# A graph layer on one core: group 0 normalised ahead of the flag, copies on VectorE from group 31, finer signals at the end

## The chip, the cores and the metric

The kernel runs on one core of a Trainium2 chip. The metric is the device time of one execution in microseconds. Three executions of the kernel before took 3143.07, 3151.29 and 3159.94 us; the median is 3151.29 us.

## What is computed

```python
h = relu(layernorm(x))                          # x: 12500 x 256, f32
agg = segment_sum(h[src], dst)                  # 200000 edges drawn, 12500 nodes
z = (1 + eps_gin) * h + agg
t = relu(batchnorm(z @ W1 + b1, g1, bt1))       # 12500 x 512
out = x + relu(batchnorm(t @ W2 + b2 + h, g2, bt2))
```

The edges are sorted by dst. Layernorm is by row; batchnorm takes its mean and variance over all 12500 rows, so that nothing of its output can be made before all of its input is there. All is f32.

## The kernel before, in words

**Tiling.** The edges are cut into 1563 tiles of 128 edges, and these into 196 groups of 8 (the last has 3). A group's rows of h are gathered into SBUF, VectorE makes a 0/1 selection matrix for it (`selection`, L712: edges x a window of 96 nodes), and TensorE sums rows into the window with 8 tiles in 16 matmuls (`aggregate`, L1228). The window is copied out of PSUM (`keep_window`, L1062), transposed (L1238) and added by VectorE into the transposed sums `aggT` (`add_window`, L789). Nodes are cut into 98 node tiles of 128, one for two groups: h of a node tile is loaded, transposed on TensorE (`transpose_h`, L1254), VectorE makes z from it (`z_tile`, L820), and the transposed h is copied over the sums, which are no longer needed (`keep_hT`, L1055). Four node tiles make a chunk of 512 nodes, 25 in all, the last of 212. `times_W1` (L1263) multiplies a chunk in 4 blocks of 128 features, one in each of four steps out of eight; `t_and_b1` (L1071) adds b1 on the way from PSUM to the buffer `tb`, VectorE takes its statistics (`t_stats`, L828), and SP stores t to DRAM (`store_t`, L451).

**Who gathers.** POOL gathers a tile of 128 rows with one indirect DMA (L606). It waits for `s_agg`, the count of summed groups, since there are 4 row buffers. In 31 groups SP fetches the eighth tile itself, row by row: it loads 16 addresses into registers (L477, a piece) and issues 16 transfers of one row of 1 KB (L482). In 24 groups from 39 on ScalarE does the same for the seventh tile (L1098, L1102). Up to group 29 the rows are those of x, and statistics, root, scale, shift and `normalise` (L1014, ScalarE) are applied to each group. Meanwhile ScalarE and VectorE also normalise x in 25 batches and store h to DRAM; from group 30 on all gathers read h (`wait_h`).

**Order.** Each engine runs its own list in the order of the code. The loop variable g of `step(g)` runs over the groups on TensorE, VectorE and ScalarE, each with its own offsets; the last four groups are written out by hand. SP's list is a loop over the 98 node tiles, here called passes: `load_node_tile(c)` (L446), which waits until node tile c - 2 has been transposed, in every fourth pass `store_t` (L451), and then the pieces of its tile, 11 quarters of a piece in a pass on average. In pass 1 it waits for the first `add_window`. ScalarE issues 5 quarters of a piece in each step, ahead of its copies of that step.

**Flag.** Early on, VectorE computes whether all edges lie within their windows (`flag`, L738). PE, ACT, POOL and DVE read it and would run a slow general path if it were 0. Group 0's statistics are taken before that and its scale, shift and normalisation after it.

**The end.** After the last sums, batchnorm 1 is finished (L933 to L942), ScalarE makes relu of a chunk (`relu1`, L1176), TensorE multiplies it by W2 in 2 blocks of 8 matmuls (`times_W2`, L1345), and VectorE adds b2 and h and takes statistics (`y_chunk`, L950 and L956). Then batchnorm 2, relu (L1187), transposes (L1359), the sum with x (`residual`, L972), and the store (L568). `keep_warm(n, bank)` (L1301) are n multiplications of the identity with itself whose result nobody reads.

```python
            def keep_window(w):                        # ScalarE
                act.wait_ge(s_agg, w + 1)
                if w >= 2:
                    act.wait_ge(s_wT, w - 1)
                S.copy(win_sb[w % 2], win_ps[w % 2]).then_inc(s_ev, 1)
...
                if c >= 2:                             # SP, load_node_tile
                    if c - 2 < H_NODES:
                        sp.wait_ge(s_hx, c - 1)
                    else:
                        sp.wait_ge(s_hT, c - 1)
```

## Time and profile before

| | before |
|---|---|
| median of three executions | 3151.29 us |
| profiled execution, its own time | 3149.71 us |
| its span, first to last instruction | 3147.9 us |
| mean granted TensorE clock | 0.72 |
| PE busy | 1454.9 us (46%) |
| POOL busy | 1431.3 us (45%) |
| VectorE (DVE) busy | 632.1 us (20%) |
| ScalarE (ACT) busy | 472.7 us (15%) |
| DMA moved | 325.72 MB, 103 GB/s |

In a profile PE is the matmuls, PEld the weight loads, and a name with q (SPq, ACTq) is an engine's queue in its role as issuer of DMAs, which isn't counted as busy. "Idle before ... <-" tells what ended an engine's idle time before an instruction: an instruction of another engine, a DMA, "issue" when the engine's queue was at something that isn't counted as busy (issuing DMAs, loading registers, fetching), and "remote" when no releaser was found. PEclk is the clock that TensorE was granted, as a share of full speed.

### The profile page before, as it was taken

To read this page: it belongs to the slowest core of one execution; us is meant where nothing else is said; L and a number is where in the kernel's file an instruction comes from. 1 tells how busy PE (TensorE), PEld (TensorE's weight loads), DVE (VectorE), ACT (ScalarE), POOL (GpSimd) and SP (SyncE) were. 2 spreads that over 40 slices of the span, in tenths; PEclk is the share of its full clock that TensorE was granted. 3 is DMA by queue.
4 is the path that set the end of the run, shared out by engine and by line. 5 is a ranking of instruction groups with operands and counts; after the bars stand their busy time and mean duration, and the time that the engine had idled before them with its cause. 6 is when DMAs were issued, how large, how long until landed. Compare 5 with 4: busy or idle time off the path is not lost.

```text
span 3147.9 us, 31339 instructions
## 1 busy us (share of the span) xinstructions
PE 1454.9 (46%) x4883; PEld 918.7 (29%) x4883; DVE 632.1 (20%) x1628; ACT 472.7 (15%) x979; POOL 1431.3 (45%) x1518
## 2 busy tenths in 40 slices
PE   2443444444434434443352453344444253444999
PEld 2222222333222222232231232222223132322546
DVE  6454531111101101111011011011011010111346
ACT  4553530000000000000000000000000000000445
POOL 5645455555444453454344544544544454553000
PEclk7766677776776776776676766767766666767999
DMA  5544432332222222222222322222322222233646
GB/s 162 169 142 145 135 111 87 93 100 79 86 87 71 87 87 78 85 87 80 75 73 84 96 71 80 83 82 87 93 74 80 76 90 80 79 92 120 235 161 255
DMA packets 129207, 325.72 MB, mean 103 GB/s; under 512 B 35641, under 2 KB 61594, under 8 KB 122862
## 3 DMA queue, kind: packets, MB, share of 16 engines
q0 software_dynamic: 72384, 197.75, 21.3%
q1 hardware_dynamic: 43946, 99.32, 8.8%
q10 hardware_dynamic: 12676, 26.68, 2.6%
q14 instruction: 162, 1.33, 0.1%
q8 instruction: 39, 0.64, 0.1%
HBM read 271.56 MB, written 52.05 MB: 103 GB/s over the span
## 4 chain that ended last, share of the span: by engine, by line
SPq 47%; issue 28%; PE 8%; ACTq 2%; another core or an unknown queue 0%; DVE 0%; ACT 0%; DVEq 0%; DMA 0%
SPq L482 38%; SPq L477 8%; PE ps L1345 5%; ACTq L1102 2%; PE ps L1359 1%; SPq L446 1%; PE ps L1301 0%; PE ps L1228 0%; PE ps L1263 0%; SPq L467 0%; SPq L451 0%; ACTq L1098 0%; DVE aggT L789 0%; DVE st L632 0%
## 5 line engine op out<-in xcount | busy, mean ns | idle before, releaser
L606 POOL DMA_INDIRECT arena<-h_rows,arena x1272 | 1205.4, 948 | 1262.9 <-PE ps L1228 755.7
L1228 PE MATMUL ps<-arena 128*96 128x256 f32 x3016 | 940.1, 478 | 754.1 <-issue 217.9
L1228 PEld LDWEIGHTS ps<-arena 128*96 128x96 f32 x3016 | 624.2, 212 | 1047.0 <-issue 619.9
L1254 PE MATMUL ps<-ident,arena 128*128 128x128 f32 x196 | 55.6, 381 | 668.7 <-ACT aggT L1055 357.5
L606 POOL DMA_INDIRECT arena<-in_x,arena x220 | 208.5, 948 | 197.2 <-PE ps L1228 112.6
L828 DVE BATCH_NORM_STATS2 arena<-arena 128x6 f32<-128x512 f32 x92 | 63.7, 693 | 1080.4 <-ACT arena L1071 788.9
L1254 PEld LDWEIGHTS ps<-ident,arena 128*128 128x128 f32 x196 | 26.8, 183 | 717.9 <-issue 685.3
L789 DVE TENSOR_TENSOR aggT<-aggT,ps 128x192 f32 x196 | 69.4, 354 | 739.6 <-PE ps L1238 357.4
L1263 PE MATMUL ps<-arena 128*128 128x512 f32 (+3 forms) x412 | 209.9, 639 | 1.3 <-DVE arena L820 1.1
L1062 ACT COPY arena<-ps 96x256 f32<-96x256 f32 x196 | 71.8, 367 | 899.1 <-issue 688.6
L1055 ACT COPY aggT<-ps 128x256 f32<-128x256 f32 x98 | 36.0, 369 | 1039.6 <-issue 1025.6
L712 DVE TENSOR_TENSOR arena<-arena,ps 128x768 f32<-128x768 f32 x196 | 185.5, 947 | 19.6 <-PE ps L1228 19.5
L1238 PE MATMUL ps<-ident,arena 96*128 96x96 f32 x392 | 68.2, 256 | 234.9 <-DVE aggT L789 180.5
L1345 PE MATMUL ps<-arena,W2s 128*128 128x512 f32 (+1 forms) x400 | 167.8, 582 | 0.0
L1014 ACT ACTIVATE arena<-arena,nb,mv 128x256 f32<-128x256 f32 x236 | 119.2, 587 | 203.5 <-DVE nb L700 127.8
L1238 PEld LDWEIGHTS ps<-ident,arena 96*128 96x128 f32 x392 | 54.8, 146 | 267.3 <-issue 228.9
L1071 ACT ACTIVATE arena<-ps,prmT 128x512 f32<-128x512 f32 (+1 forms) x100 | 67.5, 677 | 381.6 <-DMA t_T<-arena 327.9
L820 DVE SCALAR_TENSOR_TENSOR arena<-ps,eps,aggT 128x256 f32<-128x256 f32 x98 | 46.9, 480 | 364.8 <-remote 138.4
L1345 PEld LDWEIGHTS ps<-arena,W2s 128*128 128x128 f32 x400 | 75.8, 190 | 91.8 <-issue 85.9
L1263 PEld LDWEIGHTS ps<-arena 128*128 128x128 f32 x412 | 77.5, 210 | 55.7 <-issue 53.4
L632 DVE BATCH_NORM_STATS2 st<-arena 128x6 f32<-128x256 f32 x236 | 80.6, 409 | 52.1 <-DMA rl_odd<-in_x 37.8
L1176 ACT ACTIVATE arena<-arena,sh,sc 128x512 f32<-128x512 f32 (+1 forms) x100 | 72.1, 793 | 92.0 <-PE ps L1345 91.1
(94 smaller groups left out, 532.8 us busy)
## 6 DMA issues: line engine op xcount, KB each, us to landing
rl_odd<-h_rows SPq DMA_DIRECT2D x3456, 1.0 KB
W2s<-h_rows ACTq DMA_DIRECT2D x3072, 1.0 KB
t_T<-arena SPq DMA_DIRECT2D x24, 1024.0 KB, 3.8
arena<-t_T SPq DMA_DIRECT2D x24, 1024.0 KB, 4.8
arena<-h_rows,arena POOLq DMA_INDIRECT x1272
arena<-in_x SPq DMA_DIRECT2D x27, 512.0 KB, 5.6
h_rows<-arena ACTq DMA_DIRECT2D x24, 512.0 KB
out<-arena SPq DMA_DIRECT2D x23, 512.0 KB
```

The costliest lines, as they stand in the source:

```text
L477: sp.reg_load(regs, sp_at[j % 2][0:1, m * PIECE:(m + 1) * PIECE])
L482: sp.dma_start(sp_rows[j % ROW_BUFS][e:e + 1, :].bitcast(mybir.dt.uint8), a[bass.ds(at, ROW_BYTES)].rearrange("(p e) -> p e", p=1)).then_i ...
L606: nc.gpsimd.indirect_dma_start(out=rows[slot(g)][:, k, :], out_offset=None, in_=(x if g < H_FROM else h_dram)[:, :], in_offset=bass.Indire ...
L632: last = V.bn_stats(o, r)
L712: V.tensor_tensor(sel[:, g % 2, :, :], rel[:, g * GT:(g + 1) * GT].unsqueeze(2).to_broadcast([P, GT, W]), iota_ps.unsqueeze(1).to_broadcas ...
L1014: last = S.activation(rows_of(g, k), rows_of(g, k), ACT.Relu, bias=nb[:, g % 2, k:k + 1], scale=mv[:, g % 2, k, 1:2])
L1176: S.activation(u[:, k % 2, f, 0:n], tin[:, k % 2, f, 0:n], ACT.Relu, bias=sh1[:, f:f + 1], scale=sc1[:, f:f + 1]).then_inc(s_u, 1)
L1228: last = T.matmul(win_ps[g % 2], sel[:, g % 2, k, :], rows_of(g, k), start=k == 0, stop=k == n - 1)
L1238: last = T.transpose(winT_ps[:, f, :], win_sb[w % 2][:, f * P:(f + 1) * P], ident[0:W, 0:W])
L1254: last = T.transpose(hT[:, f, 0:n], h[0:n, f * P:(f + 1) * P], ident[0:n, 0:n])
L1263: last = T.matmul(t_ps[(FB * q + m) % TB][:, a:b], W1s[:, k, m * P:(m + 1) * P], zt[q % 2][:, k, a:b], start=k == 0, stop=k == DB - 1)
L1345: last = T.matmul(c_ps[k % 2][m][:, 0:n], W2s[:, f, m * P:(m + 1) * P], u[:, k % 2, f, 0:n], start=f == 0, stop=f == FB - 1)
```

## The change

- Group 0: `inverse(0)` and `shift(0)` follow `mean_and_var(0)` on VectorE, and ScalarE runs `normalise(0)` ahead of its wait for the flag; step 1 no longer holds them.
- From step 31 (`COPIES_FROM`) on `keep_window`, `keep_hT` and `t_and_b1` run on VectorE in place of ScalarE, each at its place in VectorE's step: the window copy first, the bias before the selection, the copy of hT right after the z tile. ScalarE's list has only its row issues there. The last groups, written out by hand, keep these copies on ScalarE, which waits for VectorE's last ones.
- The store of t's chunk 23 goes out after the last `add_window` in place of before it.
- `s_c` (products with W2) and `s_y` (their sums) count blocks in place of chunks.
- The last chunk's sum with x, and its store, are made in two halves.
- `keep_warm` between the last sums and the first product with W2: 4, 1, 6 and 12 in place of 8, 3, 10 and 26.
- The pieces of a pass are counted in eighths, 22 and 10, in place of quarters, 11 and 5.

```diff
@@ -37,11 +37,12 @@
 X_EARLY = 16
-SP_QUARTERS = 11
-ACT_QUARTERS = 5
+SP_EIGHTHS = 22
+ACT_EIGHTHS = 10
 H_FROM = 30
...
 HB = 4
+COPIES_FROM = H_FROM + 1
 LAST = 4
@@ -93,26 +94,26 @@
-        def quarters(q, n):
-            return q * n // 4
+        def eighths(q, n):
+            return q * n // 8
...
         while True:
-            done = ceil(4 * per_tile * (len(sp_groups) + 1), SP_QUARTERS)
+            done = ceil(8 * per_tile * (len(sp_groups) + 1), SP_EIGHTHS)
             if done > H_NODES or 2 * (done - 1) + 6 >= H_FROM:
...
         while True:
-            done = ceil(4 * per_tile * (len(sp_groups) - SP_X + 1), SP_QUARTERS) + H_NODES
+            done = ceil(8 * per_tile * (len(sp_groups) - SP_X + 1), SP_EIGHTHS) + H_NODES
             if 2 * (done - 1) + 6 >= NG - 4:
...
         while True:
-            done = ceil(4 * per_tile * (len(act_groups) + 1), ACT_QUARTERS) + H_ACT
+            done = ceil(8 * per_tile * (len(act_groups) + 1), ACT_EIGHTHS) + H_ACT
             if done - 1 + 4 >= NG - 4:
@@ -490,9 +492,9 @@
                 if c < H_NODES:
-                    return row_pieces(quarters(SP_QUARTERS, c), quarters(SP_QUARTERS, c + 1), SP_X)
+                    return row_pieces(eighths(SP_EIGHTHS, c), eighths(SP_EIGHTHS, c + 1), SP_X)
                 c -= H_NODES
-                return [(SP_X + j, m) for j, m in row_pieces(quarters(SP_QUARTERS, c), quarters(SP_QUARTERS, c + 1),
+                return [(SP_X + j, m) for j, m in row_pieces(eighths(SP_EIGHTHS, c), eighths(SP_EIGHTHS, c + 1),
                                                             len(sp_groups) - SP_X)]
@@ -527,8 +529,8 @@
             sp.dma_start(W2s[:, :, :], W2.rearrange("(k p) n -> p k n", p=P)).then_inc(s_w, 16)
+            sp.wait_ge(s_add, NG)
             store_t(NQF - 1)
-            sp.wait_ge(s_add, NG)
             for q in range(X_FIRST):
@@ -553,8 +555,8 @@
                                  (in_0, in_1, s_u, FB * (last[0] + 1)),
-                                 (at_u + 2, in_0, s_c, last[1] + 1),
-                                 (at_u, at_u + 2, s_c, last[0] + 1)):
+                                 (at_u + 2, in_0, s_c, DB * (last[1] + 1)),
+                                 (at_u, at_u + 2, s_c, DB * (last[0] + 1))):
                 for i in range(m, end):
@@ -567,9 +569,14 @@
                                  x_place(i)[a:b, :, :]).then_inc(s_o, 16)
-            for i in range(NQ):
+            for i in range(NQ - 1):
                 store_out(i)
-            sp.wait_ge(s_o, 16 * sum(len(row_parts(last_order(i)[1])) for i in range(NQ)))
+            q, n = last_order(NQ - 1)
+            for b in (0, 1):
+                sp.wait_ge(s_sum, NQ + b)
+                sp.dma_start(out[q * QN:q * QN + 4 * n, :].rearrange("(p b k) d -> p b (k d)", b=2, k=2)[:, b, :],
+                             x_place(NQ - 1)[:, b, :]).then_inc(s_o, 16)
+            sp.wait_ge(s_o, 16 * (2 + sum(len(row_parts(last_order(i)[1])) for i in range(NQ - 1))))
@@ -717,6 +724,8 @@
             mean_and_var(0)
+            inverse(0)
+            shift(0)
@@ -855,14 +864,39 @@
+            def keep_hT(c):
+                n = rows_of_node_tile(c)
+                dve.wait_ge(s_zt, c + 1)
+                dve.wait_ge(s_hTc, c)
+                hT = hT_ps if c < NT - 1 else hT_last
+                V.tensor_copy(aggT[:, :, c * P:c * P + n], hT[:, :, 0:n]).then_inc(s_hTc, 1)
+
+            def keep_window(w):
+
+                dve.wait_ge(s_agg, w + 1)
+                dve.wait_ge(s_ev, w)
+                dve.wait_ge(s_wT, w - 1)
+                V.tensor_copy(win_sb[w % 2], win_ps[w % 2]).then_inc(s_ev, 1)
+
+            def t_and_b1(q, m):
+                dve.wait_ge(s_t, FB * q + m + 1)
+                if m == 0:
+                    dve.wait_ge(s_td, 16 * q)
+                dve.wait_ge(s_tst, FB * (q - 1) + m + 1)
+                dve.wait_ge(s_tb, FB * q + m)
+                V.tensor_scalar(tb[:, m, :], t_ps[(FB * q + m) % TB][:, 0:QN], b1T[:, m:m + 1], None, ALU.add
+                                ).then_inc(s_tb, 1)
+
             def step(g):
+                if g >= COPIES_FROM:
+                    keep_window(g - 2)
                 if 2 <= g < H_FROM:
...
                     statistics_node_tile((g - 4) // 2)
-                if g <= H_FROM:
+                if 2 <= g <= H_FROM:
                     inverse(g - 1)
@@ -872,7 +906,7 @@
                     mean_and_var_node_tile((g - 4) // 2)
-                if g <= H_FROM:
+                if 2 <= g <= H_FROM:
                     shift(g - 1)
@@ -883,9 +917,14 @@
                     add_window(g - 4)
+                q, m = divmod(g - 2 * PG * Q + 1, PG * Q)
+                if g >= COPIES_FROM and m < FB:
+                    t_and_b1(q, m)
                 selection(g)
...
                     z_tile((g - 7) // 2)
+                    if g >= COPIES_FROM:
+                        keep_hT((g - 7) // 2)
                 if g - 1 < NQ:
@@ -944,13 +983,12 @@
                 n = QN if q < NQF else TAILN
-                dve.wait_ge(s_c, q + 1)
                 for f in range(DB):
+                    dve.wait_ge(s_c, DB * q + f + 1)
                     y = aggT[:, f, q * QN:q * QN + n]
-                    last = V.scalar_tensor_tensor(y, c_ps[q % 2][f][:, 0:n], b2T[:, f:f + 1], y, ALU.add, ALU.add)
-                last.then_inc(s_y, 1)
-                dve.wait_ge(s_y, q + 1)
-                for f in range(DB):
+                    V.scalar_tensor_tensor(y, c_ps[q % 2][f][:, 0:n], b2T[:, f:f + 1], y, ALU.add, ALU.add
+                                           ).then_inc(s_y, 1)
+                    dve.wait_ge(s_y, DB * q + f + 1)
                     at = 3 + 6 * (q - AHEAD2)
@@ -969,7 +1007,12 @@
                 dve.wait_ge(s_oT, i + 1)
-                V.tensor_tensor(x_place(i, n), o_ps[i % 2][0:n, :, :], x_place(i, n), ALU.add).then_inc(s_sum, 1)
+                if i < NQ - 1:
+                    V.tensor_tensor(x_place(i, n), o_ps[i % 2][0:n, :, :], x_place(i, n), ALU.add).then_inc(s_sum, 1)
+                else:
+                    for b in (0, 1):
+                        z = x_place(i, n)[:, b, :]
+                        V.tensor_tensor(z, o_ps[i % 2][0:n, b, :], z, ALU.add).then_inc(s_sum, 1)
             for i in range(NQ):
@@ -1073,6 +1116,7 @@
             zero_step(2)
+            normalise(0)
             act.wait_ge(s_flag, 1)
@@ -1112,27 +1156,27 @@
                     load_batch(g)
-                if g <= H_FROM:
+                if 2 <= g <= H_FROM:
                     normalise(g - 1)
...
                 if g >= H_ACT:
-                    for j, m in row_pieces(quarters(ACT_QUARTERS, g - H_ACT), quarters(ACT_QUARTERS, g - H_ACT + 1),
+                    for j, m in row_pieces(eighths(ACT_EIGHTHS, g - H_ACT), eighths(ACT_EIGHTHS, g - H_ACT + 1),
                                            len(act_groups)):
...
                         root_node_tile((g - 4) // 2)
-                    if g >= 8:
+                    if 8 <= g < COPIES_FROM:
                         keep_hT((g - 8) // 2)
-                if g >= 2:
+                if 2 <= g < COPIES_FROM:
                     keep_window(g - 2)
...
                 q, m = divmod(g - 2 * PG * Q + 1, PG * Q)
-                if q >= 0 and m < FB:
+                if q >= 0 and m < FB and g < COPIES_FROM:
                     t_and_b1(q, m)
@@ -1142,8 +1186,10 @@
+            act.wait_ge(s_ev, a - 2)
+            act.wait_ge(s_hTc, c - 1)
+            act.wait_ge(s_tb, FB * q + 1)
             keep_window(a - 2)
-            keep_hT(c - 2)
             t_and_b1(q, 1)
@@ -1171,7 +1217,7 @@
                 if at_least(q, 2):
-                    act.wait_ge(s_c, q - 1)
+                    act.wait_ge(s_c, DB * (q - 1))
                 for f in range(FB):
@@ -1324,27 +1370,27 @@
             pe.wait_ge(s_tb, FB * NQF - TB + 1)
-            keep_warm(8, idle)
+            keep_warm(4, idle)
             aggregate(a + 3)
-            keep_warm(3, idle)
+            keep_warm(1, idle)
             transpose_window(a + 3)
-            keep_warm(10, idle)
+            keep_warm(6, idle)
             for m in range(FB):
                 times_W1(NQF, m)
-            keep_warm(26, 1)
+            keep_warm(12, 1)
...
             def times_W2(q, k, r, n=QN):
-                if at_least(q, 2):
-                    pe.wait_ge(s_y, q - 1)
                 for m in range(DB):
+                    if at_least(q, 2):
+                        pe.wait_ge(s_y, DB * (q - 2) + m + 1)
                     for f in range(FB):
...
                                         start=f == 0, stop=f == FB - 1)
-                last.then_inc(s_c, 1)
+                    last.then_inc(s_c, 1)
             chunks(pe, 4, NQF, times_W2, lambda q, k, r: times_W2(q, k, r, TAILN))
```

## Rows read from the trace of the kernel before

**Rows 1.** Busy time by engine in one stretch (number of instructions behind x)
```profile
core 0: us, PE busy (x) PEld busy (x) DVE busy (x) ACT busy (x) POOL busy (x), PEclk, DMA share, GB/s
...
522.40:2877.60 2355.20, 984.96 (x3254) 631.54 (x3254) 278.20 (x467) 130.44 (x311) 1140.68 (x1204) 0.69 0.28 83
```
**Rows 2.** The page's chain by line, and SP's own waits in the whole span
```profile
SPq L482 38%; SPq L477 8%; PE ps L1345 5%; ACTq L1102 2%; PE ps L1359 1%; SPq L446 1%; PE ps L1301 0%; PE ps L1228 0%; PE ps L1263 0%; SPq L467 0%; SPq L451 0%; ACTq L1098 0%; DVE aggT L789 0%; DVE st L632 0%
...
SPq L446 <- DVE aggT L789: 26.6, 1, 26.6
...
SPq L446 <- PE ps L1254: 9.7, 1, 9.7
```
**Rows 3.** Stretches from one node-tile load to the next: POOL's gathers (L606)
```profile
1141.09:1184.28 43.19, 28.89 (x31) 0.73 0.33 97
2308.72:2336.04 27.32, 17.14 (x19) 0.80 0.30 89
2336.04:2365.23 29.19, 15.66 (x17) 0.68 0.28 83
2402.52:2424.16 21.64, 0.00 (x0) 0.50 0.17 64
2611.37:2646.53 35.16, 17.21 (x19) 0.79 0.24 70
2823.21:2864.79 41.58, 28.26 (x30) 0.66 0.34 99
```
**Rows 4.** Waits from 530 to 2877 us, and L1062's group there
```profile
PE ps L1254 <- ACT aggT L1055: 343.1, 36, 21.5
...
PE ps L1228 <- ACT arena L1062: 157.5, 27, 15.4
...
L1062 ACT COPY arena<-ps 96x256 f32<-96x256 f32 x157 | 57.8, 369 | 855.2 <-issue 667.0 <-PE ps L1238 95.5 <-remote 80.8
```
**Rows 5.** Timeline: start, us, row issues and a gather; L1102's first and last start
```profile
1154.89 11.52 ACTq L1102 DMA_DIRECT2D W2s<-h_rows  x17
...
L1102 ACTq DMA_DIRECT2D W2s<-h_rows x3072: 2/235/1412, 444.9 to 2748.2; - x192
...
2310.40 10.23 SPq L482 DMA_DIRECT2D rl_odd<-h_rows  x14
...
2319.93 5.63 SPq L482 DMA_DIRECT2D rl_odd<-h_rows  x3
...
2332.18 0.95 POOL L606 DMA_INDIRECT arena<-h_rows,arena  x1 [3.71 <-remote]
...
2337.69 8.87 SPq L482 DMA_DIRECT2D rl_odd<-h_rows  x16
```
**Rows 6.** Timeline: a wait for a t store, and the last such store
```profile
2407.08 0.69 ACT L1071 ACTIVATE arena<-ps,prmT 128x512 f32<-128x512 f32 x1 [23.31 <-DMA t_T<-arena]
...
2878.99 0.43 SPq L451 DMA_DIRECT2D t_T<-arena  x1
...
2889.51 0.69 ACT L1071 ACTIVATE arena<-ps,prmT 128x512 f32<-128x512 f32 x1 [34.76 <-DMA t_T<-arena]
```
**Rows 7.** Timeline: the flag, the first sums, the fifth gather, the first window added
```profile
46.66 0.14 DVE L738 TENSOR_SCALAR flag<-flag_f 1x1 int32<-1x1 f32 x1 [9.55 <-remote]
...
55.08 5.46 PE L1228 MATMUL ps<-arena 128*96 128x256 f32 x16 [20.63 <-ACT arena L1014]
...
61.35 0.94 POOL L606 DMA_INDIRECT arena<-in_x,arena  x1 [16.92 <-PE ps L1228]
...
84.12 0.35 DVE L789 TENSOR_TENSOR aggT<-aggT,ps 128x192 f32 x1 [7.39 <-remote]
```
**Rows 8.** Timeline: warming, first relus, first products with W2
```profile
2929.68 5.97 PE L1301 MATMUL ps<-ident 128*128 128x128 f32 x52
...
2932.38 5.75 ACT L1176 ACTIVATE arena<-arena,sh,sc 128x512 f32<-128x512 f32 x8 [0.84 <-DVE sh L942]
...
2935.49 25.06 PE L1345 MATMUL ps<-arena,W2s 128*128 128x512 f32 x58
```
**Rows 9.** Timeline: sums of the tail chunk, and the last residual
```profile
3103.36 0.78 DVE L950 SCALAR_TENSOR_TENSOR aggT<-ps,prmT,aggT 128x212 f32<-128x212 f32 x2
...
3142.08 1.23 DVE L972 TENSOR_TENSOR aggT<-ps,aggT 128x1024 f32<-128x1024 f32 x1 [0.18 <-PE ps L1359]
```

More of the change, by code:

```diff
@@ L200, in build @@
         W1s = piece[1].rearrange("p (k n) -> p k n", n=F)
+        assert COPIES_FROM % 2 == 1 and COPIES_FROM > max(H_ACT, 2 * H_NODES + 2, NQ + 2)
         W2s = sb("W2s", [P, FB, D])
```

## The prediction

> **What bounds the kernel now.** I read the stages first, then which queue never waits, then what slows that queue. The gather stage runs from 452.6 to 2877.6 us; in its 2355 us from 522.4 on PE is busy 42%, VectorE and ScalarE 12% and 6%, and POOL, the highest, 48% of the time [rows 1]. No engine is full. The chain of waits puts 38% of the span on SP's queue at L482, the issue of one-row transfers [rows 2]. SP's own waits confirm it: two matter, 26.6 us for the first window sum and 9.7 us for a transpose of TensorE, and in the stretch 522.4 to 2877.6 us there is none [rows 2]. So SP is never late because of anyone: whoever else waits there waits in SP's shadow.
>
> What sets SP's pace is seen by cutting the stage into passes (node-tile load to node-tile load, two groups each, 32 or 48 one-row transfers, 2.75 pieces of 16 on average). A pass of 48 rows takes 21.64 us when POOL gathers nothing in it, 35.16 us with 19 gathers, 41.58 and 43.19 us with 30 and 31; one of 32 rows takes 27.32 us with 19 [rows 3]. That is (41.58 - 21.64) / 30 = 0.66 us for a gather and 21.64 / 48 = 0.45 us for a row. The diff leaves both counts as they are: 22 eighths of a piece are 11 quarters, 10 eighths are 5 quarters. So the stage keeps its length unless SP begins to wait or the gathers fall otherwise in time.
>
> **ScalarE's copies.** From group 31 VectorE takes over 157 window copies of 369 ns and the copies and biases at L1055 and L1071. TensorE now waits 343.1 us for L1055 and 157.5 us for L1062 there [rows 4], because these copies stand behind bursts of row issues in ScalarE's queue. Those 500 us go, but TensorE then waits for the next node tile or SP's rows, which come no sooner: worth nothing on the path. VectorE has room for the copies, some 140 us of busy time in a stretch in which it is busy 278 of 2355 us [rows 1, 4]. What does come off is SP's own wait: its pass due at 512.4 us starts at 522.4 because TensorE's transpose waits for L1055 and L1062 behind ScalarE's issues. **Minus 9.7 us** [rows 2]; bounds 0 (something else holds the transpose) and 9.7.
>
> ScalarE, freed, issues its rows with fewer pauses. The trace shows whether that robs SP: the pass of 43.19 us had 31 gathers and 17 rows of ScalarE in one row of the timeline alone, the pass of 41.58 us had 30 gathers and came after ScalarE's last row at 2748.2 us [rows 3, 5]. Less the one gather of 0.66 us, 0.95 us is left for at least 17 rows, at most 0.06 us each; ScalarE's total stays the same, so I take nothing. The Trainium skill ("DMA: Bandwidth & Descriptors", section "Issuing engines are not separate DMA queues") says that transfers of all issuers end on the same 16 engines and interleave; if ScalarE's rows cost SP as much as SP's own, the two passes should lie 17 x 0.45 = 7.7 us apart, and they lie 1.61 us apart.
>
> **The wait that moves to VectorE.** The bias of block 0 waits until the previous t store has landed, and SP issues that store only at the start of a later pass. ScalarE stood 23.31 us in such a wait [rows 6], and VectorE's statistics stand behind it even now. Now VectorE itself stands there, and selection of group 8q+15, the z tile and the copy of hT are queued behind it; TensorE misses one group more before the block ends, and POOL one release. SP asks for a transpose two node tiles back, so it has about two passes (60 us) of slack against a delay of about one group (some 10 us of gathers): nothing, 19 times. The last block has no pass after it: the store goes out at 2878.99 behind two 1 MB loads and ScalarE resumes at 2889.51 [rows 6]; selection of group 191 now waits for that, where its sums ran at 2886. Between 0 and 5 us, of which later stalls of up to 6 us may hide part: **plus 2 us**.
>
> **Group 0.** Its normalisation comes after the flag (46.66 us), and TensorE's first sums start at 55.08 after 20.63 us of waiting; POOL's fifth group then starts at 61.35 after 16.92 us [rows 7]. Normalised before the flag (ScalarE is free from 30 us), the sums can start about 49 us, so POOL starts 6 us sooner. The groups after it gain less, since VectorE's scale and shift for group 1 come only 0.4 us sooner. SP's second pass hangs on the first window sum at 84.12 [rows 7] and nothing but transfers follows it, so what arrives there is kept: between 0 and 6, **minus 4 us**.
>
> **Warming.** 26 calls are 52 matmuls of L1301 and take 5.97 us, 0.23 us each [rows 8]. The first four calls removed lie between sums (-0.9 us); of the next, two are hidden behind the last window copy; four before W1 give 0.6 us until the z tiles are there; 14 of the last 26 calls would give 3.2 us, but the first product can't precede the first of 8 relus, which start at 2932.38 and take 0.72 us each, where TensorE started at 2935.49 [rows 8]: -2.3 us. **Minus 3.8 us**, if the clock stays at the 1.00 of that stretch; if it fell to half for the first chunk, 6.7 us of products would cost 6.7 more.
>
> **Small ends.** Signals per block let VectorE take block 0 of the tail chunk while TensorE makes block 1: the first of the two sums (0.78 us for both) and its statistics, a little shorter, go beside it: **-0.6 us** [rows 9]. For the other chunks TensorE never waits, so nothing. The last residual takes 1.23 us before its store [rows 9]; in halves the first store goes out 0.6 us sooner, the second carries half as much but VectorE pays a second start of some 0.1 us: -1.1 to +0.3, **-0.5 us**. The t store behind the last sums is needed at chunk 6 at the earliest: 0.
>
> **Sum.** The profiled execution took 3149.7 us (span 3147.9), the median is 3151.3. -9.7 + 2 - 4 - 3.8 - 0.6 - 0.5 = -16.6: **3133 us**, 0.58% under the median. A measurement of this kernel can tell about 0.5% from no change, so the borders are 3135.5 and 3167.0 us, and the forecast lies just past the first.
>
> **Rivals.**
> 1. *Gathers broken up more.* SP's cost for a gather isn't constant: two passes of 48 rows took 29.19 us with 17 gathers and 35.16 us with 19 [rows 3]. Before and within the first POOL stopped between groups, once for 3.71 us, and SP issued 16 rows in 8.87 us; in a long stretch of gathers it issued 14 rows in the first 10.23 us and then 3 in 5.63 us [rows 5]. Long unbroken stretches cost SP more. If TensorE at SP's heels leaves POOL in catching-up mode, in which it breaks after every 8 gathers, I let one of 8 of the 79 passes turn from unbroken to split: 10 x 5 = -50 us (5 us is the 5.97 between the two passes less 2 gathers at the 0.44 of a split pass, (29.19 - 21.64) / 17): 3083 us.
> 2. *Slower: gathers bunched.* The same rows in the other direction. ScalarE's bursts of rows now space TensorE's groups, and POOL, which waits for each, gathers in pieces. With prompt copies two groups follow each other closely, and POOL can gather 16 tiles without a break in each pass. It decides if more than about one pass in twenty changes from split to unbroken (4 passes x 5 us pay back the gain). If a quarter of 79 passes change, 20 x 5 = +100 us: 3235 us.
> 3. *No gain in the middle.* SP's wait at 512 us only moves, or the time is given back in the tail: 3149.7 - 7 = 3143 us.
> 4. *The copies were the bound*: TensorE's 500 us of waits for them come off in part, say half: 2900 us. Against it speaks that SP's queue has no wait in 2355 us.
>
> **Chances.** Forecast's own case 0.45 (3118 to 3148; six tenths of it under 3135.5), rival 1 0.18, rival 2 0.15, rival 3 0.17, rival 4 0.05. Faster by over 0.5%: 0.27 + 0.18 + 0.05 = 0.50; within: 0.18 + 0.17 = 0.35; slower 0.15. The range takes in rival 1 and stops short of rival 2: 3080 to 3180 us, leaving out rivals 2 and 4 (0.20).
>
> **What would show it.** SP without a wait in the stretch and the pass at 512 us on time; copies on VectorE and TensorE's waits turned to SP's rows and node tiles; the first window sum near 80 us; TensorE's first product near 2932 less the shift. Passes with 16 gathers at 35 us throughout would show rival 2, at 29 us rival 1. SP waiting at L446 once in four passes would show that VectorE's wait for the t store reached it, which would make the prediction wrong.

## The result: 1.3% slower

The changed kernel takes 3188.33 us (median of four, 3182.24 to 3194.64), the kernel before 3148.12 us on the same chip: ratio 1.0126, 95% interval 1.0090 to 1.0162. The forecast was 3133 us, 0.6% faster; the time lies above the range too (3080 to 3180 us). The profiled execution took 3194.64 us, 44.9 more than that of before.

The page of the changed kernel: span, busy time, chain of waits by engine and by line.

```profile
span 3192.7 us, 31384 instructions
...
PE 1377.2 (43%) x4835; PEld 878.9 (28%) x4835; DVE 778.1 (24%) x1952; ACT 337.3 (11%) x656; POOL 1428.0 (45%) x1518
...
SPq 57%; issue 32%; PE 8%; DMA 0%; DVE 0%; ACT 0%; DVEq 0%; ACTq 0%
SPq L484 46%; SPq L479 9%; PE ps L1391 5%; PE ps L1405 1%; SPq L448 1%; PE ps L1274 1%; PE ps L1309 0%; DMA t_T<-arena 0%; SPq L453 0%; SPq L469 0%; ACT arena L1057 0%; PE ps L1347 0%; PE ps L1284 0%; DMA arena<-in_x 0%; DVE st L639 0%
```

L484 is the old L482, SP's issue of single rows: 46% of the chain instead of 38% [rows 2]. The same two kinds of instruction bound the kernel, only more so. SP's waits for TensorE and for the first window:

```profile
SPq L448 <- PE ps L1300: 34.2, 3, 19.5
...
SPq L448 <- DVE aggT L798: 18.7, 1, 18.7
```

All of them lie before 430 us; from the start of the gather stage to 2923 us SP never waits. The wait of 9.7 us that was to go is gone, and yet its pass starts 31 us later. Busy time of the two passes before it, from 452.61 us in the kernel before and from 453.83 us in the changed one (columns as in [rows 1]), and of the rest of the gather stage of the changed kernel:

```profile
452.61:522.41 69.80, 37.23 (x133) 24.08 (x131) 11.20 (x20) 9.21 (x21) 39.65 (x43) 0.78 0.29 86
```
```profile
453.83:553.47 99.64, 54.89 (x187) 35.50 (x187) 22.37 (x45) 5.37 (x12) 63.72 (x68) 0.76 0.32 94
```
```profile
553.50:2923.20 2369.70, 893.46 (x3200) 583.91 (x3198) 405.85 (x763) 0.00 (x0) 1117.39 (x1182) 0.68 0.27 82
```

The two passes hold 80 rows of SP in both kernels, but POOL now gathers 67 tiles in them instead of 42, and they take 99.6 us instead of 69.8. Against [rows 1], the stretch after them is 2369.70 us instead of 2355.20. So the loss is 30 us in the two passes that follow the change to h and 14 us spread over the passes after them. Start and tail together come out 1 us longer: plus 1.2 us before pass 14, plus 6.1 from pass 92 to the last gather, minus 6.6 after it.

VectorE's wait for the t store, summed over 530 to 2923 us and once in the timeline:

```profile
DVE arena L887 <- DMA t_T<-arena: 765.1, 19, 53.7
...
POOL arena L613 <- PE ps L1274: 737.7, 59, 33.7
```
```profile
1098.43 0.75 DVE L887 TENSOR_SCALAR arena<-ps,prmT 128x512 f32<-128x512 f32 x1 [36.40 <-DMA t_T<-arena]
```

In the kernel before it was ScalarE that stood there, from 530 to 2877 us:

```profile
ACT arena L1071 <- DMA t_T<-arena: 293.1, 16, 23.3
```

That is 18 us on average, 16 times; VectorE, which reaches the place sooner, stands 40 us on average, 19 times.

The copies on VectorE don't slow the gathers themselves: one takes 0.946 us in the changed kernel and 0.949 in the one before, and in a train they follow each other every 1.25 us in both.

### The profile page after: what moved, and what is told of

Same layout as the page of the kernel before. It is cut to its first block, busy times and chain, and to the rows that moved or that the text cites. A ratio compares the mean times of both kernels' runs of the same rounds, so it can differ in the third digit from the quotient of the medians.

```text
span 3192.7 us, 31384 instructions
## 1 busy us (share of the span) xinstructions
PE 1377.2 (43%) x4835; PEld 878.9 (28%) x4835; DVE 778.1 (24%) x1952; ACT 337.3 (11%) x656; POOL 1428.0 (45%) x1518
## 3 DMA queue, kind: packets, MB, share of 16 engines
q14 instruction: 164, 1.34, 0.1%
## 4 chain that ended last, share of the span: by engine, by line
SPq 57%; issue 32%; PE 8%; DMA 0%; DVE 0%; ACT 0%; DVEq 0%; ACTq 0%
SPq L484 46%; SPq L479 9%; PE ps L1391 5%; PE ps L1405 1%; SPq L448 1%; PE ps L1274 1%; PE ps L1309 0%; DMA t_T<-arena 0%; SPq L453 0%; SPq L469 0%; ACT arena L1057 0%; PE ps L1347 0%; PE ps L1284 0%; DMA arena<-in_x 0%; DVE st L639 0%
## 5 line engine op out<-in xcount | busy, mean ns | idle before, releaser
L1274 PE MATMUL ps<-arena 128*96 128x256 f32 x3016 | 889.4, 458 | 935.7 <-issue 438.9
L1274 PEld LDWEIGHTS ps<-arena 128*96 128x96 f32 x3016 | 596.0, 203 | 1197.0 <-issue 980.4
L879 DVE COPY arena<-ps 96x256 f32<-96x256 f32 x161 | 67.4, 419 | 934.7 <-remote 504.6
L1105 ACT COPY arena<-ps 96x256 f32<-96x256 f32 x35 | 12.6, 359 | 2476.7 <-DVE aggT L872 2450.7
L887 DVE TENSOR_SCALAR arena<-ps,prmT 128x512 f32<-128x512 f32 x81 | 60.6, 748 | 867.9 <-DMA t_T<-arena 801.4
L1309 PE MATMUL ps<-arena 128*128 128x512 f32 (+3 forms) x412 | 200.0, 614 | 1.6 <-DVE arena L829 1.5
L798 DVE TENSOR_TENSOR aggT<-aggT,ps 128x192 f32 x196 | 67.8, 346 | 83.2 <-issue 38.5
```

What stands on the lines that cost most here:

```text
L1274: last = T.matmul(win_ps[g % 2], sel[:, g % 2, k, :], rows_of(g, k), start=k == 0, stop=k == n - 1)
L1309: last = T.matmul(t_ps[(FB * q + m) % TB][:, a:b], W1s[:, k, m * P:(m + 1) * P], zt[q % 2][:, k, a:b], start=k == 0, stop=k == DB - 1)
```

## How the stage is counted

The trace's timeline was cut in one way for all kernels: from pass 14 to pass 92 of SP (453 to some 2900 us), which always holds 3450 issues of SP (3424 rows and 26 loads of addresses, called rows below), 3078 of ScalarE (3056 and 22), and 1557 to 1565 us of gathering. A gather is counted with the 0.3 us that follow it, and gathers with less than 0.6 us between them then form a train. "Beyond 10" is the part of the gathering that lies over 10 us into a train. The columns on rows count those issued while POOL gathers. The chips on which single rows are slow are called stalling chips below, those on which they aren't, even chips.

The table has one execution of each kernel, all on stalling chips, from four timings, each on one chip: before and changed; r2, e6 and e7; e11, e9 and e8; e15. The kernel before itself differs by 38 us of stage and 52 rows between the first two, so rows are held against each other within one timing, except for e15, which has no partner in its own. The ratio is that of the medians to the kernel before in the same timing.

| kernel | ratio | stage us | gathering, of it beyond 10 | pauses | SP's rows in gathering | ScalarE's |
|---|---|---|---|---|---|---|
| before, first chip | 1 | 2412 | 1560, 513 | 852 | 1712 | 1594 |
| changed, first chip | 1.0126 | 2456 | 1562, 529 | 894 | 1656 | 1607 |
| before again (r2) | 0.9975 | 2450 | 1565, 544 | 885 | 1660 | 1561 |
| loose pace (e6) | 1.0125 | 2492 | 1563, 548 | 928 | 1601 | 1651 |
| old pace (e7) | 1.0186 | 2509 | 1562, 539 | 947 | 1553 | 1665 |
| copies back (e11) | 1.0012 | 2414 | 1558, 518 | 856 | 1716 | 1605 |
| t on ScalarE (e9) | 1.0066 | 2439 | 1557, 588 | 882 | 1664 | 1604 |
| held twice (e8) | 1.0140 | 2470 | 1562, 557 | 907 | 1604 | 1688 |
| t stores by ScalarE (e15) | 1.0414 | 2559 | 1563, 751 | 996 | 1391 | 1515 |

The gathering is a constant. What SP hasn't issued by its end it issues in the pauses, at 2.0 to 2.1 rows per us: (3450 - 1656) / 894 = 2.01, (3450 - 1391) / 996 = 2.07. So **a row that SP doesn't get out while POOL gathers costs half a microsecond**. For the change: 56 rows x 0.5 = 28 us; the pauses' own rate fell from 2.04 to 2.01, 14 us more; gathering 2: together the 44 us.

In the first 10 us of a train SP and ScalarE together issue 2.67 to 2.79 rows per us, beyond it 0.83 to 0.96, in the pauses 3.5 to 3.8, in every one of these runs. SP therefore loses rows when the gathers fall into longer trains or when ScalarE has a larger share. The two don't make up the 56 rows of the change. The 16 us more beyond 10 are some 15 rows: 16 x (1.40 - 0.47), SP's own rates within and beyond the first 10 us. The rest is mostly a lower rate of SP within the first 10 us, 1.35 rows per us instead of 1.40 (r2 has 1.37), while ScalarE's rate there stays at 1.34. No run here shows where that comes from.

The two parts of the stage differ. In passes 14 and 15 the gathering beyond 10 us grows from 1.6 to 47.5 us, which is the bunching. From pass 16 to 92 it shrinks, from 511.6 to 481.3 us.

## The experiments

The kernel before was run beside each of them.

**1. Copies back on ScalarE.** All the rest of the change stays.

```
-COPIES_FROM = H_FROM + 1
+COPIES_FROM = 201          # (and ScalarE makes the copy of hT in its tail again)
```

> The changed kernel with all of ScalarE's copies put back (VectorE takes none); group 0, the warming, the signals per block, the store order and the halves stay as changed. Theory A (the copies on VectorE lengthen the gather stage, by about 44 us of the profiled span, while the rest is worth about nothing or a few us less): 3135 to 3150 us, ratio to the kernel before 0.996 to 1.001. Rival C (the loss lies in the other edits, for instance the start that shifts all later passes): 3175 to 3195 us, as the changed kernel.

Measured: 2116.15 us against 2125.16, ratio 0.9958 (0.9945 to 0.9972). The surprise is the 2125: on this chip the kernel before is 1000 us faster. Below is SP's row issue of the changed kernel on such a chip (run later) and on the first chip, over the same 18.4 us, both with POOL gathering for all or most of it: line, queue, operation, count, then duration in ns least/median/most.

```profile
L484 SPq MOVE rl_odd<-h_rows x45: 29/29/29, 534.3 to 552.0; - x45
L484 SPq DMA_DIRECT2D rl_odd<-h_rows x45: 227/228/299, 534.4 to 552.1; - x45
```
```profile
L484 SPq DMA_DIRECT2D rl_odd<-h_rows x11: 3/698/1397, 533.9 to 551.8; - x11
L484 SPq MOVE rl_odd<-h_rows x11: 3/29/716, 534.6 to 552.2; - x11
```

45 rows against 11. And the MOVE, which sets a register and moves no data, takes up to 0.72 us where it takes 0.029 us on the fast one (over the whole run up to 1.45 us). So the delay isn't one of the row transfers alone: SP's own instructions come late. On this even chip SP isn't the bound; in e1 POOL gathers without a pause.

**2. Copies from group 61, ScalarE at its old pace, POOL draining.** Three more on this even chip.

```
+COPIES_FROM = H_FROM + 31                      # e2
+elif g >= COPIES_FROM: act.wait_ge(s_ev, g - 1)    # e3, in ScalarE's step
+wait_apart(pool, s_rows[(g - 1) % RG], ...)    # e4: group g - 1 has landed
```

> The changed kernel with the copies taken over by VectorE from group 61 on instead of 31, so that the catching-up stretch after the change to h (pass 14 to 18, 453 to 600 us) runs as before. In the profiled runs the passes 14 and 15 carry about 30 of the 45 us lost. If the loss is made in that stretch: 3150 to 3165 us. If it is made by a steady cost of each pass that merely happened to fall early: 3175 to 3190 us. If it is lost on a chance pattern of gathers anywhere, the place of the loss moves to the passes after 30 and the total stays near 3180.

> The changed kernel, copies on VectorE, but ScalarE waits at each group for the window copy that it used to make itself, so its row transfers keep the pace of before (bursts of 16 to 97) instead of running up to 400 us in one train. Theory A (prompt copies let POOL gather without breaks and that slows SP): no change, 3175 to 3195 us. Theory B (ScalarE's rows, issued in long trains and ahead of time, take the transfers' time from SP): the loss goes, 3140 to 3160 us.

> The changed kernel with one more wait: from group 31 on POOL starts the gathers of a group only when those of the group before have landed, so no stretch of gathers goes beyond 8. Theory A (long unbroken stretches cost SP about 5 us each where they replace two short ones; about 39 stretches of 14 and more gathers in the changed kernel): 39 x 5 = up to 190 us less if POOL never becomes late, 3000 to 3120 us. Rival B or C: no gain, 3180 us or more, since POOL only loses time.

Measured: 1.0076 (1.0062 to 1.0090), 0.9954 (0.9940 to 0.9967) and 1.2086 (1.2070 to 1.2103). The first says nothing on where the first chip lost, since here POOL sets the pace and not SP; the last makes POOL wait 495 us for its own landings and tests nothing where POOL is the bound. The middle one stands out: with its old pace the kernel takes the 2116 us of experiment 1, though all copies are on VectorE.

**3. The changed kernel on an even chip, and the old pace again.**

> The changed kernel as it is, on the chip of this call. In the first call the kernel before took 2125 us where it took 3148 us when the change was timed. If the chip is again one on which POOL never stops (2125 us): by theory B (ScalarE's rows running ahead of their pace) the changed kernel takes 2135 to 2165 us, ratio 1.005 to 1.02, as with copies from group 61 (1.0076) or a little more; by theory A (prompt copies join the gathers) it takes 2105 to 2125 us, since there the gathers are joined anyway. If it is a chip like the first (3148 us): 3175 to 3200 us.

> Again the changed kernel in which ScalarE waits at each group for the window copy that it used to make, so that its rows keep their pace. Where POOL never stops: 2110 to 2120 us, ratio 0.9954 as measured. If the chip is one of 3148 us: theory B says that the loss goes there too, 3130 to 3160 us; theory A that it stays, 3175 to 3200 us.

Measured: 1.0060 (1.0047 to 1.0074) and 0.9956 (0.9943 to 0.9970). Here the change loses too, for a reason that the pace removes. Waits of TensorE and POOL from 352 to 1866 us, first as changed, then with the old pace:

```profile
PE ps L1274 <- DMA arena<-h_rows,arena: 338.1, 83, 8.6
PE ps L1274 <- DMA rl_odd<-h_rows: 117.0, 15, 17.0
...
POOL arena L613 <- PE ps L1274: 29.9, 32, 7.2
```
```profile
PE ps L1276 <- DMA arena<-h_rows,arena: 542.7, 135, 8.0
...
POOL arena L613 <- PE ps L1276: 6.1, 20, 0.3
```

As changed, ScalarE issues its first 2048 rows almost without a pause. From pass 44 to 60 it issues 715 rows beside SP instead of 640, SP's mean interval from row to row within a piece grows from 0.331 to 0.342 us, and the 16 passes take 324.2 us instead of 309.8, which is POOL's own time (248 gathers x 1.25 = 310). SP's rows come late, TensorE waits 117 us for them, and POOL stops for 24 us more; the 21 us between the two runs are that.

**4. Three kernels on a stalling chip.** The next chip was of the first kind (before: 3192.54 us).

```
+elif g >= COPIES_FROM + 6: act.wait_ge(s_ev, g - 7)    # e6
```

e7 is e3 with inverse(0), shift(0) and normalise(0) back behind the flag.

> The kernel before itself, for its trace on the chip of this call. On a chip as in the two calls so far: 2123 to 2128 us, POOL without a pause from the first pass to the end of the gathers, SP's pass of 48 rows near 21 us whatever POOL does. On a chip as that of the first timing: 3140 to 3160 us, passes of 48 rows between 21 and 43 us.

> The changed kernel with ScalarE held to VectorE's window copies, but six groups looser than in the run with the old pace, so its rows may run six groups (at most 120 rows) ahead. Theory B in the form 'what counts is how long ScalarE issues without a pause beside SP': the ratio lies between that of the old pace (0.9955) and that of the changed kernel (1.006), near the old pace, since the lead is used up once and then ScalarE is paced again: 0.995 to 0.999. If instead any lead of ScalarE's rows over the copies costs the full price (the order within a group counts): 1.003 to 1.007.

> The changed kernel with the old pace of ScalarE, and group 0 normalised after the flag as in the kernel before. If the early normalisation is worth what the prediction gave it (4 us): 2119 to 2121 us where the paced kernel took 2116, ratio 0.997 to 0.998. If the start is hidden elsewhere: 0.9955, unchanged. On a chip of 3148 us, theory B gives 3135 to 3165 us for it and theory A 3175 to 3205 us.

Measured: 0.9975 (0.9955 to 0.9995), 1.0125 (1.0093 to 1.0157), 1.0186 (1.0145 to 1.0228). The first is the same kernel as its partner, and its interval leaves out 1, so these comparisons are good to about 0.3% and no better. ScalarE's pace, all of the loss on an even chip, is none of it here: with the old pace (and group 0 late) the loss is no smaller. As a ratio that is just above the range of theory A. And the lengths of the trains don't explain e7 either (539 us beyond 10 against 544); in its row of the table ScalarE has 104 rows more in the gathering and SP 107 fewer, 107 x 0.5 = 54 of the 58 us between the stages.

**5. Who stands in the wait for the t store.** On a third stalling chip (before: 3147.57 us).

```
+elif q >= 1 and m == 0: act.wait_ge(s_td, 16 * q)   # e8: e3, and ScalarE waits there too
-if g >= COPIES_FROM and m < FB: t_and_b1(q, m)      # e9: e3, VectorE's; ScalarE keeps it
```

> The changed kernel with ScalarE held at each group for the window copy and, once for each t block, for the landing of the t store, as before the change; all the copies are on VectorE. On a chip where the kernel before takes 3148 to 3192 us: theory S (ScalarE's freed time goes into rows issued within the gathers' stretches, at SP's expense) gives ratio 0.99 to 1.003; theory V (VectorE's wait for the t store stops selection, TensorE and POOL) gives 1.01 to 1.02, as with the pace alone (1.0186). On a chip of 2125 us: 0.995 to 0.997 by both, as with the pace alone.

> The changed kernel with the old pace, in which only the window copies and the copies of hT are on VectorE; the t blocks with their wait for the store stay on ScalarE. On a chip of 3148 to 3192 us: both S and V give 0.99 to 1.003, S because ScalarE stands in the wait again, V because VectorE doesn't. If it stays at 1.01 or more, the window copies alone make the loss. On a chip of 2125 us: 0.995 to 0.997.

> All the change but the copies, again. On a chip of 3148 to 3192 us: S and V both say that the loss is gone, 0.994 to 1.0; a loss of 1% would mean that it comes from the start or from another edit. On a chip of 2125 us: 0.9958 as before.

Measured: 1.0140 (1.0092 to 1.0188), 1.0066 (1.0038 to 1.0094), 1.0012 (0.9984 to 1.0040). Without the copies no loss is seen: it is the copies, not the start or the tail (the changed kernel itself wasn't run on this chip; e8 stands for it). About half of it comes with the window copies and hT (e9, which neither theory had), the rest with the t blocks. e8 spoke for VectorE's wait as the cause, and against ScalarE's freedom in the form in which it can be undone by holding it at the old places.

The passes tell where the second half lies. Passes 14 and 15 hold 42 to 48 gathers and take 67 to 78 us in every kernel whose t blocks are on ScalarE (before, r2, e11, e9), and 63 to 69 gathers and 93 to 102 us in every kernel whose t blocks are on VectorE (changed, e6, e7, e8, e15). Between e9 and e8 that is 27 of the 31 us of the stage. So the 30 us in two passes come with the t blocks and not with the window copies. In the passes after them the changed kernel, e6, e7, e8 and e9 all lose, 14 to 36 us (e9 19).

**6. VectorE's wait taken away.** ScalarE issues the t stores as soon as VectorE has filled a block.

```
+if g >= 35 and (g - 19) % 8 == 0:                  # ScalarE's step, after the old pace
+    act.wait_ge(s_tb, FB * ((g - 19) // 8 + 1))
+    act.dma_start(t_dram[(g - 19) // 8, :, :, :], tb[:, :, :]).then_inc(s_td, 16)
```

> The changed kernel with ScalarE at its old pace, and the t stores 2 to 21 issued by ScalarE as soon as VectorE has filled the block, not by SP at the start of a later pass, so VectorE finds the store landed. All copies are on VectorE. On a chip of 3148 to 3192 us: if the wait for the store carries the loss beyond that of the window copies (1.0186 or 1.014 with it on VectorE, 1.0066 with it on ScalarE), the ratio is 1.000 to 1.008; if not, 1.012 to 1.02. On a chip of 2125 us: 0.993 to 0.996.

That and a repetition fell on even chips: 0.9954 (0.9940 to 0.9967) and 0.9957 (0.9943 to 0.9971). The third time it was a stalling one.

> The changed kernel with ScalarE at its old pace and the t stores issued by ScalarE, a third time. On a chip of 3148 to 3192 us: if the wait for the store carries the loss beyond that of the window copies, 1.000 to 1.008; if not, 1.012 to 1.02. On a chip of 2125 us: 0.9955.

Measured: 1.0414 (1.0380 to 1.0447), 3292.16 us against 3159.04, outside both ranges. So the wait for the store isn't what makes the loss; in this kernel it seems to be a brake that does good. The edit also moves the issue of the stores from SP to ScalarE and has ScalarE wait for each full block, so the wait alone isn't tested. The gather stage of e15, 545.97 to 3024.7 us:

```profile
POOL arena L614 <- PE ps L1280: 870.7, 47, 39.1
PE ps L1306 <- DMA arena<-h_rows: 836.2, 47, 28.3
DVE arena L880 <- PE ps L1290: 578.5, 56, 30.4
...
DVE arena L888 <- DMA t_T<-arena: 22.8, 1, 22.8
```

One wait for a store is left, TensorE follows SP's loads of node tiles at its heels, and POOL gathers in 82 trains, 76 of them of 14 tiles or more, where with the copies back (e11, on another chip) it is 107 and 55. 751 us of gathering lie beyond 10 us into a train instead of 518: 233 us in which SP issues 0.48 instead of some 1.4 rows per us, about 210 of the 325 rows that it lacks.

**7. Fewer single rows.** Copies on ScalarE as in e1.

```
-SP_EIGHTHS = 22
-ACT_EIGHTHS = 10
+SP_EIGHTHS = 11            # e10; 5 in e13 and e16
+ACT_EIGHTHS = 5            # e10; 2 in e13 and e16
```

> All the change but the copies, with half as many single-row transfers (SP 11 and ScalarE 5 eighths of a piece per pass and per group instead of 22 and 10); POOL gathers 1536 tiles instead of 1508. On a chip of 3148 to 3192 us, if single rows are what SP's pace is made of (0.45 us each, 0.66 for a gather): 22 x 0.45 + 15.7 x 0.66 = 20.3 us for a pass, about POOL's own 15.7 x 1.25 = 19.6, so the stage falls from some 31 us a pass to 20 to 23: 2200 to 2500 us. On a chip of 2125 us, where POOL never stops: 28 x 1.25 = 35 us more than 2116, 2150 us, ratio 1.012.

> All the change but the copies, with SP at 5 and ScalarE at 2 eighths of a piece (6 and 4 tiles by single rows instead of 31 and 24); POOL gathers 1553 tiles. On a chip of 3148 to 3192 us, by the account: a pass 10 x 0.45 + 15.8 x 0.66 = 15 us of SP's time, under POOL's 15.8 x 1.25 = 19.8 us, so POOL becomes the bound: 1553 x 1.25 = 1941 us and some 250 to 300 us around it, 2190 to 2300 us, ratio 0.70 to 0.73. On a chip of 2125 us: 45 more gathers than 1508 at 1.25 us, 2172 us, ratio 1.022.

> All the change but the copies, with 6 and 4 tiles by single rows instead of 31 and 24, again. On a chip of 3148 to 3192 us, by the account of rows against gathers: POOL becomes the bound, 2190 to 2300 us, ratio 0.69 to 0.73; if the chip slows the gathers themselves too, 2350 to 2550 us. On a chip of 2125 us: 2171 us, ratio 1.0214.

Measured: half the rows, on a stalling chip, 2574.93 us against 3147.57, ratio 0.8188 (0.8153 to 0.8222); few rows, on an even chip, 2171.44 us, 1.0214 (1.0200 to 1.0228), as 45 x 1.25 us says; on a stalling chip 2502.46 us against 3159.04, 0.7924 (0.7896 to 0.7952). So on chips as that on which the change was timed few rows beat the kernel before by a fifth, and on an even chip they lose 2%. Both stopped short of the account (2200 to 2500 us for half the rows, 2190 to 2300 for few). POOL's waits in e16 from 446.1 to 2160.8 us and a piece of its timeline:

```profile
POOL arena L613 <- issue: 350.5, 1125, 1.9
POOL arena L613 <- remote: 209.5, 46, 6.2
POOL arena L613 <- PE ps L1272: 39.8, 14, 6.2
```
```profile
1009.37 0.33 PE L1282 MATMUL ps<-ident,arena 96*128 96x96 f32 x2
...
1012.65 21.78 SPq L484 DMA_DIRECT2D rl_odd<-h_rows  x16
...
1027.52 0.94 POOL L613 DMA_INDIRECT arena<-h_rows,arena  x1 [0.30 <-issue]
1032.80 0.37 ACT L1105 COPY arena<-ps 96x256 f32<-96x256 f32 x1 [23.80 <-remote]
1032.85 0.35 DVE L798 TENSOR_TENSOR aggT<-aggT,ps 128x192 f32 x1 [24.25 <-remote]
...
1033.35 0.56 PE L1282 MATMUL ps<-ident,arena 96*128 96x96 f32 x2 [18.41 <-DVE aggT L798]
1033.47 0.94 POOL L613 DMA_INDIRECT arena<-h_rows,arena  x1 [5.01 <-remote]
```

Even 16 rows take 21.78 us under a long train. And late in a train it is not SP alone that stalls. TensorE's transposes of a window (L1282) end at 1009.70; VectorE's addition of that window (L798) and ScalarE's next window copy (L1105) have nothing else to wait for and start at 1032.85 and 1032.80, 4 us after POOL's last gather. TensorE in turn waits for both, and POOL for TensorE's signal of a sum that was over before 1015. The trace has this all through e16: of the 68 additions whose transposes end later than 8 us into a train, 54 start over 2 us late with VectorE idle, 13 us late on average over the 68; of 152 in e13, the same kernel on an even chip, none. POOL's 249 us of such waits are most of what keeps e16 above the 2171 us of e13.

## Why the prediction was wrong

**What bounds the kernel: right, but the unit was wrong.** On the first chip SP bounds the stage and never waits in it, before and after. But the prediction priced a pass by the number of its gathers and rows, 0.66 and 0.45 us, and closed with "the stage keeps its length unless SP begins to wait or the gathers fall otherwise in time". The second is what happened, and in the direction of slower it was given 0.15.

**Minus 9.7 us for the pass at 512 us: this step failed most.** The wait went, as forecast. But TensorE's lateness at 512 us seems to have kept POOL short of free slots, too. In the changed kernel POOL gathers 25 tiles more in those two passes, 32 us of gathering in which SP gets few rows: plus 29.8 where minus 9.7 was put. By e9 it is the t blocks on VectorE that bring this, which the prediction took for free together with the other copies. The 21 gathers that fall away after pass 16 bring 30 us less gathering, but 67 fewer rows of SP in it and so 45 us more pauses: plus 14. What is late next was asked for SP's wait only, not for SP's pace.

**"I take nothing" for ScalarE's rows.** The bound of 0.06 us for a row came from two passes that differ in at least 17 rows of ScalarE (32 by the trace); but the prediction itself shows two passes that lie 5.97 us apart with two gathers between them, so a single pair bounds nothing this small. On an even chip 75 rows of ScalarE more beside SP lengthen 16 passes by 14.4 us, 0.19 us each (r1 against e5). On a stalling one the number doesn't matter (3078 always) but the place does: in e7 against r2 ScalarE has 104 rows more within gathering and SP 107 fewer. In the change itself ScalarE has only 13 more, so this step is a smaller part of the 44 us. The Trainium skill ("DMA: Bandwidth & Descriptors", section "Issuing engines are not separate DMA queues") says that transfers of all issuers end on the same 16 engines. The row traded for a row agrees with that; the MOVE of up to 1.45 us, which transfers nothing, speaks for a limit ahead of the transfers on these chips.

**The wait that moves to VectorE.** Estimated at one group, some 10 us, hidden. It is 40 us on average. What it costs inside the stage can't be told by itself: with the t blocks and their wait on ScalarE the ratio is 1.0066 instead of 1.0140, and with the wait taken away by e15's edit 1.0414. SP never waits for it, as forecast. At the last block the estimate was plus 2:

```profile
2924.75 0.43 SPq L453 DMA_DIRECT2D t_T<-arena  x1
...
2931.62 0.94 POOL L613 DMA_INDIRECT arena<-h_rows,arena  x1 [23.20 <-PE ps L1274]
...
2935.52 0.75 DVE L887 TENSOR_SCALAR arena<-ps,prmT 128x512 f32<-128x512 f32 x1 [36.26 <-DMA t_T<-arena]
```

From pass 92 to the last gather it takes 38.4 us instead of 32.3: plus 6, and POOL waits there for TensorE, as the step said. The other runs bear it out: 38.6 to 39.0 us in e6, e7 and e8, 32.7 to 34.0 with the copies back (e11), with the t blocks on ScalarE (e9) or with ScalarE's stores (e15).

**Group 0.** TensorE's first sums start at 50.31 instead of 55.08, POOL goes on at 57.55 instead of 61.35, the first window is added near 76 instead of 84 [rows 7], and by pass 4 nothing is left (191.4 us against 189.8). On stalling chips pass 2 starts at 121.8 to 128.3 us with it and at 123.3 to 123.9 without. The minus 4 isn't shown; whether it exists on an even chip wasn't measured by itself.

**Warming and small ends.** Last window added to first product: 10.3 us before, 7.6 after: minus 2.7, forecast for that place minus 2.9 (0.6 ahead of the products with W1, 2.3 behind them).

```profile
2978.76 2.40 PE L1347 MATMUL ps<-ident 128*128 128x128 f32 x20
...
2981.01 3.63 ACT L1222 ACTIVATE arena<-arena,sh,sc 128x512 f32<-128x512 f32 x5 [0.83 <-DVE sh L981]
...
2981.97 2.38 PE L1391 MATMUL ps<-arena,W2s 128*128 128x512 f32 x5 [0.81 <-ACT arena L1222]
```

The clock stayed at 1.00 there. The last residual and its stores end 4.8 us after TensorE's last operation instead of 5.9: minus 1.1, the optimistic bound, where minus 0.5 was taken.

```profile
3188.03 1.29 DVE L1015 TENSOR_TENSOR aggT<-ps,aggT 128x512 f32<-128x512 f32 x2 [0.18 <-PE ps L1405]
3188.75 0.93 SPq L577 DMA_DIRECT2D out<-aggT  x2
```

From the last gather to the end it is 244.2 us instead of 250.8: minus 6.6 for all of them, forecast minus 4.9. Together with group 0 these terms are all that e1 and e11 have: minus 9 us on an even chip; on a stalling one minus 5.5 from the last gather on (against the first chip's trace), where the total can't tell it from nothing.

**The rivals.** Rival 2 had the mechanism of passes 14 and 15: gathers follow one another without a break. It put it in a quarter of all passes, at 100 us. In the other passes of the change it doesn't come: trains of 14 tiles or more fall from 53 to 46 there. In e15 it comes as described, in 72 trains, and the loss is 133 us. Rival 1, the opposite sign of the same mechanism, was given more chance than it, 0.18, on no better evidence.

**What stays open.** Why SP's rate early in the trains falls in the changed kernel. Why, with the old pace, ScalarE's rows move into the gathering when VectorE copies. Later than 12 us into a pause ScalarE issues 1.4 to 1.8 rows per us in the kernels with VectorE's copies, 1.9 to 2.0 in those without, so it seems to be held there by what waits for TensorE and to make up for it beside POOL; that is argued from the counts, not shown by a run. Why the t blocks on VectorE let POOL run ahead in passes 14 and 15. And why one chip stalls instructions and signals under gathers and another doesn't. The recording itself isn't ruled out: on stalling chips the traces lack part of the signals (178 instead of 196 for TensorE's transposes of windows and 136 for VectorE's selections, before; e1 has 194 and 197), and every execution that was timed was recorded at least for its span.

## What to carry to other kernels

If a queue bounds a stage and its speed depends on what runs beside it, count how much it gets done beside each neighbour, and price every edit by that count; a stall removed elsewhere is no gain if it starts a neighbour earlier. A wait off the critical path may be a brake that helps the bound engine: take it away in an experiment before calling it waste. Where the bound is how fast one-row issues go, try fewer of them before moving anything around them. And before explaining half a percent, run the kernel against itself on another chip.

## What the runs showed of the hardware

The kernel before takes 2125 to 2126 us on two chips and 3148 to 3193 us on three others and where the change was first timed, with the same 0.95 us for a gather. The difference shows in SP's and ScalarE's own instructions while POOL gathers: on an even chip SP's MOVE is 0.029 us always (r1); on a stalling one it averages 0.11 us in the first 8 us of a train and 0.38 us after it in the kernel before, 0.44 in the changed one.

It shows in the signals between engines too. In the changed kernel VectorE's window copy waits for nothing but TensorE. For 57 copies both the inputs and VectorE's queue are ready later than 4 us into a train; 49 of them start over 2 us after that. Of the 53 such late copies in all trains 40 start only after the train has ended. On an even chip 1 copy of 144 is late (r1). So on a stalling chip a long train of gathers holds up every engine that depends on another, and POOL itself once it runs out of released buffers.

The sign of an edit can turn between the two kinds of chip: one and the same kernel gave 0.9954 and 0.9957 on even chips and 1.0414 on a stalling one (e12, e14, e15); few rows cost 2% on one and save 21% on the other. A kernel with many one-row issues beside indirect gathers has to be timed on both.
